# A first stage in units of two tiles that stores only z, with the transposed rows made during the walk

## The reference

```
xn   = (x - mean) / sqrt(var + 1e-5)                      # per row of x
neigh_mean = segment_sum(xn[src], dst) / max(deg, 1)      # 100000 edges, dst sorted
gnn  = relu(concat([xn, neigh_mean]) @ W + b), rows scaled to norm 1
mix  = linear attention of rmsnorm(xn) * g_pre:
       q, k, v = that @ w_qkv; softmax(k) over the nodes, softmax(q) over a head
       out = rmsnorm((context q) @ w_out + b_out, g_out) + xn
x    = x + gnn + mix
x    = x + moe(layernorm(x))                              # 8 experts, top 2, gelu
```

## Time and profile before

| | us |
|---|---|
| median of 3 executions | 2344.38 (2333.13 to 2353.49) |
| the profiled execution | 2353.81 |
| its span in the profile | 2352.2 |
| start of the first gather of the walk | 122.6 |
| first stage and tables: share of the span | 5% |

### The profile page before, as it was taken

The page is one execution under the profiler, slowest core; times in us unless marked ns, Lnnn a source line. Parts: engine busy times, 40 slices in busy tenths (PEclk is TensorE's granted clock), DMA queues, the critical chain, the costliest instruction groups (busy, mean ns, idle before and its releaser), DMA issues.

```text
span 2352.2 us, 34761 instructions
## 1 busy us (share of the span) xinstructions
PE 1657.8 (70%) x9472; PEld 1336.8 (57%) x9473; DVE 1372.5 (58%) x3837; ACT 594.3 (25%) x1554; POOL 1209.1 (51%) x1199
## 2 busy tenths in 40 slices
PE   2855666565556566787666544434999999999998
PEld 2633434343335344433434334424999999999997
DVE  7843444343335466776777567642666666666664
ACT  0200000000000133323433337521333333333332
POOL 4366676666666566656666534553333333333333
PEclk8966777677777777898787775556999999999999
DMA  7833333333332366666666547546776776777665
GB/s 212 283 104 98 99 105 100 98 103 101 103 103 81 115 222 197 200 177 187 200 196 191 164 122 258 181 131 158 197 200 194 191 199 197 190 194 200 196 188 152
DMA packets 203694, 387.28 MB, mean 165 GB/s; under 512 B 34677, under 2 KB 148362, under 8 KB 189015
## 3 DMA queue, kind: packets, MB, share of 16 engines
q0 software_dynamic: 77520, 258.14, 39.0%
q1 hardware_dynamic: 116448, 125.08, 17.0%
q10 hardware_dynamic: 9638, 3.13, 0.6%
HBM read 302.36 MB, written 84.67 MB: 165 GB/s over the span
## 4 chain that ended last, share of the span: by engine, by line
PE 48%; issue 15%; another core or an unknown queue 13%; DVE 12%; DMA 6%; POOL 3%; DVEq 1%; ACT 1%; SPq 1%; POOLq 0%; ACTq 0%
PE bank L1724 16%; PE bank L1574 11%; PE bank L1740 4%; PE bank L1742 4%; PE bank L1741 4%; DVE acc_lent L1156 4%; PE bank L1616 2%; DMA w1s<-in_x_dram 2%; PE bank L1582 1%; POOL G L626 1%; PE bank L1714 1%; PE bank L1631 1%; DMA xTs<-xnT_d 1%; POOL w2s_lent L626 1%
## 5 line engine op out<-in xcount | busy, mean ns | idle before, releaser
L1156 DVE TENSOR_TENSOR acc_lent<-acc_lent,bank 128x258 f32 x832 | 349.6, 420 | 531.0 <-remote 248.7
L626 POOL DMA_INDIRECT w2s_lent<-z_d,edge_tabs_lent x416 | 407.4, 979 | 234.5 <-issue 115.4
L626 POOL DMA_INDIRECT G<-z_d,edge_tabs_lent x416 | 408.6, 982 | 222.2 <-issue 118.1
L1574 PE MATMUL bank<-G,S_lent 128*128 128x258 f32 x832 | 308.3, 502 | 221.4 <-issue 114.3
L1724 PE MATMUL bank<-acc_lent 128*128 128x128 f32 x3392 | 398.2, 276 | 0.5 <-DVE acc_lent L1462 0.5
L1724 PEld LDWEIGHTS bank<-acc_lent 128*128 128x128 f32 x3392 | 390.2, 193 | 0.9 <-issue 0.9
L1574 PEld LDWEIGHTS bank<-G,S_lent 128*128 128x128 f32 x832 | 185.5, 245 | 333.6 <-issue 213.1
L909 ACT ACTIVATE G<-bank,acc_lent 128x128 f32<-128x128 f32 x848 | 242.6, 369 | 522.9 <-PE bank L1724 522.9
L1574 PE MATMUL bank<-w2s_lent 128*128 128x258 f32 x832 | 265.8, 447 | 129.3 <-issue 81.8
L1574 PEld LDWEIGHTS bank<-w2s_lent 128*128 128x128 f32 x832 | 163.6, 216 | 223.0 <-issue 152.7
L683 POOL DMA_INDIRECT out_dram<-acc_lent x106 | 170.4, 1607 | 187.5 <-DVE acc_lent L1468 172.9
(11 more groups left out here) (274 smaller groups left out, 2422.0 us busy)
## 6 DMA issues: line engine op xcount, KB each, us to landing
acc<-w2lo_d POOLq DMA_DIRECT2D x106, 1024.0 KB, 5.2
acc_lent<-bucket_d SPq DMA_DIRECT2D x106, 133.0 KB, 2.6
xTs<-xnT_d SPq DMA_DIRECT2D x98, 128.0 KB
bu_d<-w2s_lent SPq DMA_DIRECT2D x98, 128.0 KB
w2s_lent<-bu_d SPq DMA_DIRECT2D x14, 768.0 KB
w1s<-in_L_ffn_W_dram SPq DMA_DIRECT2D x8, 1024.0 KB
w2s_lent<-in_L_ffn_W_dram SPq DMA_DIRECT2D x32, 256.0 KB
w2hi_d<-w2s_lent SPq DMA_DIRECT2D x32, 256.0 KB
```

Source lines behind the costliest of these rows:

```text
L626: pool.indirect_dma_start(out=G_half[half][:, k, 0:D], out_offset=None, in_=z_d[:, :], in_offset=bass.IndirectOffsetOnAxis(ap=srcT[:, step ...
L1156: dve.tensor_tensor(to, to, bank[k % 4][:, 0:ACCW], ALU.add).then_inc(s["acc_done"], 1)
L1574: pe.matmul(bank[k % 4][:, 0:ACCW], S_half[half][:, k // S_GROUP, k % S_GROUP, :], G_half[half][:, k, :], start=True, stop=True).then_inc( ...
```

## The change

- **Units.** The first stage works on 25 units (LN_UNITS) of two tiles, with three buffers each for xn, xnT, zs. x is loaded by two tiles at a time with 8 loads outstanding (before: three tiles, 2 outstanding).
- **Who does what.** DVE writes mean and variance straight from bn_aggr, ACT's root adds eps through a bias pointer, DVE makes rstd and -mean*rstd (`scales`), and ACT normalises by an activation with scale and bias from pointers, one per tile. z is copied from PSUM by ACT for even units, by DVE for odd ones.
- **Stores.** Only z is stored in the first stage. POOL's additions and s_d are dropped.
- **Order at the start.** Units 0 to 5 (LN_BEFORE = 5) come ahead of the sort check. POOL clears acc after the 7 indirect DMAs. Of the weights only g_pre and w_kv are loaded here; ACT issues the other 17 DMAs one per tile in the first part of the walk, and DVE uses them in blocks 26 to 30 at step 3.
- **Walk, first part.** Per tile ACT normalises again from x_all (L706) into xr, PE transposes (`turn_a`, at step 2, two transposes), ACT copies into xTs (L806), and SP stores xTs to xnT_d (L435) where it loaded before.
- **Walk, last part.** SP loads x into sB; ACT makes s = x*(1 + rstd) - mean*rstd there (`make_s`), between `norm_o` and `copy_qT`; DVE waits for it.

The diff, cut to its core:

```diff
@@ first stage, SP
-            units(load_x, sp, None)
...
+            for n in range(LN_UNITS):
+                t0, nt = tiles_of(n)
+                until(sp, x_in[n % X_AHEAD], 16 * (n // X_AHEAD))
...
+            for n in range(9):
+                store_z(n)
...
-            def store_unit(i, h, t0, nt):
-                sp.wait_ge(pair["s_ready"][h], i + 1)
-                sp.dma_start(s_t[:, ds(t0, nt), :], ss[h][:, 0:nt, :]).then_inc(pair["s_out"][h], 16)
-                sp.wait_ge(pair["xnT_ready"][h], i + 1)
-                sp.dma_start(xnT_t[:, ds(t0, nt), :], xnT[h][:, 0:nt, :]).then_inc(pair["xnT_out"][h], 16)
...
             for t in range(NT):
+                sp.wait_ge(s["xa_ready"], t + 1)
+                sp.dma_start(xnT_d[t], xTs[:, :]).then_inc(s["xa_out"], 16)
@@ POOL
-            pool.memset(acc_flat, 0.0).then_inc(s["consts_pool"], 1)
...
             sort_places()
             step_rows()
-            with pool.Fori(1, UN) as i:
-                adds(i)
-            add_unit(UN, 0, NT - 1, 1)
+            pool.memset(acc_flat, 0.0).then_inc(s["consts_pool"], 1)
@@ ACT
+            def norm_x(to, t):
+                return act.activation(to, x_all[:, t, :], ACT.Identity, scale=rstd[:, t:t + 1], bias=mean_var[:, t, 0:1])
...
+            def ln_step(n):
+                if n + 1 < LN_UNITS:
+                    unit_sd(n + 1)
+                unit_xn(n)
+                if n >= 1:
+                    unit_xnT(n - 1)
+                if n >= 2 and n % 2 == 0:
+                    unit_z(n - 2)
...
             for t in range(NT):
+                if t < NT - 1:
+                    norm_a(t + 1)
                 kv(t)
+                if t < NT - 1:
+                    copy_a(t + 1)
+                next(weights, None)
...
+            def make_s(t):
+                act.wait_ge(s["sb_in"], 16 * (t + 1))
+                act.activation(sB[:, :], sB[:, :], ACT.Identity, scale=rstd1[:, t:t + 1], bias=mean_var[:, t, 0:1]).then_inc(s["s_made"], 1)
...
             def mix(t):
                 exp_q(t)
                 norm_o(t - 1)
+                make_s(t - 1)
                 copy_qT(t)
@@ DVE
-            def norm_iter(i, first=False, last=False):
-                norm_unit(i, 0, 6 * i, 3)
-                stats(i + 1, 0, 6 * i + 6, 1 if last else 3)
-                if not first:
-                    z_unit(i - 1, 0, 3)
...
+            for n in range(LN_BEFORE + 1, LN_UNITS + 1):
+                if n < LN_UNITS:
+                    stats(n)
+                if n % 2:
+                    z_unit(n - 2)
+                if n < LN_UNITS:
+                    scales(n)
+                if n == LN_BEFORE + 2:
+                    dve.wait_ge(s["kv_weights_in"], 16 * (DC + 1))
```

More of the change, by code:

```diff
@@ L456, in io_b @@
                     store_b(t - 1)
[L457 removed]
+                    load_s(t)
             def io_load(t, to, frm):
@@ new lines, in unit_sd, with unit_xn @@
+            def unit_sd(n):
+                t0, nt = tiles_of(n)
+                act.wait_ge(s["var_ready"], n + 1)
+                act.activation(rstd[:, t0:t0 + nt], mean_var[:, t0:t0 + nt, 1], ACT.Sqrt, bias=eps_ln).then_inc(s["ln_sd"], 1)
+            def norm_x(to, t):
+                return act.activation(to, x_all[:, t, :], ACT.Identity, scale=rstd[:, t:t + 1], bias=mean_var[:, t, 0:1])
+            def unit_xn(n):
+                t0, nt = tiles_of(n)
+                act.wait_ge(s["ln_ready"], n + 1)
+                until(act, s["xnT_mm"], n + 1 - LN_BUFS)
+                for tt in range(nt):
+                    a = norm_x(xn[n % LN_BUFS][:, tt, :], t0 + tt)
+                a.then_inc(s["xn_ready"], 1)
@@ new lines, in unit_xnT, with unit_z @@
+            def unit_xnT(n):
+                nt = tiles_of(n)[1]
+                h = n % LN_BUFS
+                act.wait_ge(s["xnT_mm"], n + 1)
+                until(act, s["z_mm"], n + 1 - LN_BUFS)
+                act.activation(xnT[h][:, 0:nt, :], x_bank[h][:, 0:nt * D].rearrange("p (t d) -> p t d", d=D),
+                               ACT.Copy).then_inc(s["xnT_ready"], 1)
+            def unit_z(n):
+                nt = tiles_of(n)[1]
+                h = n % LN_BUFS
+                act.wait_ge(s["z_mm"], n + 1)
+                until(act, z_out[h], 16 * (n // LN_BUFS))
+                act.activation(zs[h][:, 0:nt, :], z_bank[h][:, 0:nt * D].rearrange("p (t d) -> p t d", d=D),
+                               ACT.Copy).then_inc(s["z_copied"], 1)
@@ L777, in _ @@
                 act.dma_start(ed[0:EP], edges_d.rearrange("(p j) k e -> p j k e", j=EJ)).then_inc(s["edges_in_again"], 16)
-            repeat(act, None, copies, 1, UN - 1)
-            copy_xnT(UN - 1, 0, 3)
-            unit_sd(UN, 0, NT - 1, 1)
-            copy_xnT(UN - 1, 1, 3)
-            copy_xnT(UN, 0, 1)
-            act.wait_ge(s["rstd_ready"], 1)
-            act.activation(r16[:, :], t49, ACT.Sqrt).then_inc(s["sd_ready"], 1)
+            unit_sd(LN_BEFORE + 1)
+            for n in range(LN_BEFORE + 1, LN_UNITS):
+                ln_step(n)
@@ L787, in kv, with norm_a, copy_a @@
+            def norm_a(t):
+                until(act, s["xaT_mm"], t)
+                norm_x(xr, t).then_inc(s["xa_norm"], 1)
+            def copy_a(t):
+                act.wait_ge(s["xaT_mm"], t + 1)
+                until(act, s["kv_mm"], t)
+                until(act, s["xa_out"], 16 * t)
+                act.activation(xTs[:, :], bank[7][:, 0:D], ACT.Copy).then_inc(s["xa_ready"], 1)
             def kv(t):
@@ new lines, in stats, with scales @@
+                a.then_inc(s["var_ready"], 1)
+            def scales(n):
+                t0, nt = tiles_of(n)
+                r = rstd[:, t0:t0 + nt]
+                dve.wait_ge(s["ln_sd"], n + 1)
+                L.after(dve.reciprocal(r, r))
+                mean = mean_var[:, t0:t0 + nt, 0:1]
+                dve.scalar_tensor_tensor(out=mean, in0=mean, scalar=-1.0, in1=r.rearrange("p (t o) -> p t o", o=1),
+                                         op0=ALU.mult, op1=ALU.mult).then_inc(s["ln_ready"], 1)
@@ L1113, in _ @@
-            z_unit(UN, 0, 1)
-            rstd = mean_rstd[:, 1, 0:NT]
-            L.after(dve.tensor_tensor(t49, var49, rstd, ALU.mult))
-            L.after(dve.tensor_tensor(t49, t49, rstd, ALU.mult))
-            dve.tensor_scalar(t49, t49, float(D), None, ALU.mult).then_inc(s["rstd_ready"], 1)
+            for n in range(LN_BEFORE + 1):
+                stats(n)
+                if n >= 1:
+                    scales(n - 1)
+            scales(LN_BEFORE)
+            z_unit(1)
+            step_tables()
```

399 lines of the change are left out of this document (189 added, 210 removed).

## The result

The changed kernel takes 2386.7 us (median of 4, 2381.3 to 2392.3) against 2342.5 of the kernel before (four runs of it by now): ratio 1.020, interval 1.017 to 1.023. It is 44 us slower; 2375 was forecast.

A forecast was written before the change was run, and what follows sets the result against it. It took the old first stage's steady part as DVE-bound at 1.50 us a tile, the walk as bound by no single engine. Stage 14, clock 8, clearing 4, walk 1 and 4 gave +31 on 2344.4: 2375 us, range 2325 to 2410.

The forecast's parts named there:

- The chain: First stage's loop: steps wait on one another round all engines, 8.25 us a pair of units, no engine full.
- The rival that the loop isn't a chain: First stage's loop: signals overlap, PE bounds at 2.42 us a unit; total 2330 to 2325 us; chance 0.16.
- The stage's sum: First stage: its pieces add up to a first gather at 136.4 us against 122.6, +14 us.
- The forecast's own sign: End of first stage: the walk's first gather would show at 136 us, within 123 to 165.
- The start: Before the loop: PE's sort check matmul stands behind five units, at 35.4 us, 9.1 later; DVE resumes at about 44.9.
- The clearing: POOL's clearing of acc, now inside the first stage's loop, may hold DVE's scaling of w_kv: +4 us, bounds 0 and +10.9.
- Clock: First stage's loop: PE's idle time in each pair lowers its granted clock: +8 us, bounds 0 and +25.
- Half clock throughout: Rival: PE stays at 1.2 GHz in the whole first stage, pair 11.0 us, total 2392 us; chance 0.10.
- The first round: First stage, after DVE resumes: unit 6 through its first round, charged as half a pair, 4.4 us.
- The tables: First stage's loop: casting and subtracting steps, 0.6 and 1.45 us, plus two pairs of table copies of 1.76: 5.6 us.
- The walk: After the first stage: added transposes and normalisations +1 us in its first part, making s +4 in its last.
- that rival (2300): Walk's first part gets faster without xTs's load, up to 74 us back, total 2300 us; chance 0.14.

The follow-up runs named there:

- the best version: Changed kernel with clearing at start, odd z copy later, normalisation before root, LN_BEFORE 3, earlier W_neigh load, tables' steps spread: 2134.0 us (0.995), again 2128.7 (0.994).
- the filled version: Changed kernel with 6 extra, unused PE matmuls at even steps of the first stage's loop, not at the tables' steps: 2187.8 us, ratio 1.020.
- the version with the three edits: Changed kernel with acc cleared at the start, odd units' z copy one step later on DVE, ACT's normalisation ahead of the next root: 2341.3 us, ratio 1.0005.
- the version with the late z copy: Changed kernel with DVE copying z of odd units one step later, acc clearing left late: 2352.4 us, ratio 1.004.

## Why the prediction was right, point by point

- **The chain: right, and shown.** Forecast 8.25 us a pair, measured 8.07 at full clock. That the lengths agree to 0.2 is partly luck, since the forecast added 2.75 us of PE to two rounds of DVE and ACT, and the trace shows 4.7 us of PE and one round. Moving one copy made it 5.90, moving the root as well 4.92. The rival that the loop isn't a chain (2325 to 2330) falls: its first gather of 103 is approached only once the order is edited (113.1, and 104.1 and 106.3 in the best version).
- **The stage's sum: 136.4 forecast, 168.2 measured, with clock and clearing 148.** The forecast's own sign, a first gather from 123 to 165, was missed. The start is 3.1 late: PE waited 6.9 us for W_neigh, which the forecast had landed by 18.4, though the five units then took 13.0 and not 17. Its load was issued at 13.98 and took 11.7 us, where it was issued at 11.0 before and took 7.1; why it took longer was not tested. From DVE's return to its first z copy it is 8.5 and not 4.4. The nine intervals between z copies (56.50 to 163.65) take 107.2 against 74.3 + 5.6. The end is 2.6 shorter.
- **The clearing: mechanism right, term too small.** +4 forecast inside bounds of 0 and 10.9; the multiply was held for 11.05, 10.4 more than its 0.61. It began 0.2 us behind the clearing, so nothing of it was over: the argument that DVE would come late to it was a guess.
- **Clock: right in kind, mis-sized where the loop had long pauses.** +8 was forecast. Outside of the tables' pairs I count 9: 1.6 ahead of the first z copy (PE's part of that way is 4.1 us and 2.5 at full clock), 2.5 behind the clearing, and 5.0 in three of the last five pairs, beside the filled version. In the tables' pairs PE's pieces of the chain take 19.1 us; by the plain pairs and by the best version's transposes of the steps (0.93 for seven) they would take about 11 at full clock, an estimate. So the clock took some 17 us in all, twice the charge. Half clock throughout (2392) did not come to be, since pairs at full clock stand among the others, and its nearness to 2386.7 is luck.
- **The first round: charged half a pair, 4.4.** It takes 8.5, of which 1.6 is the clock. DVE and ACT go through two rounds before PE may start on the newest unit, so 2.5 were missing; the scaling's own 0.6 stood in no term either.
- **The tables: the step that failed.** I charged their own work, 5.6 us, and left them out of the chain. DVE's wait for PE's transposes of the steps stands ahead of the next unit's statistics, as the z copy does. The two pairs take 19.8 and 12.9 us, 16.6 over two plain pairs, so 11 beyond the charge. By the estimate above some 8 of the 11 are the low clock of these two pairs and 3 are the wait and the transposes on PE; that the pauses brought the low clock is argued here, since these pairs were filled only in part. Other profiles of the same stage show 30.3 to 32.7 us for the two, so 9 to 11 beyond the charge. In the version with the three edits, at full clock, the tables cost 3.3 beyond it. Apart by two units and behind the loop's slack they cost the best version 5.5, which is the charge.
- **The walk: charged 5, measured 0 to 3.** Its first part did not get faster either (564.7 to 564.2 us), though xTs's load left it: that rival (2300) falls, and the load was not what holds the blocks at 12 us. What does was not looked for.
- **The total.** Sum of the terms as measured: 14 + 3 (start) + 3 (first round and scaling) + 10 (clearing, on +0) + 9 (clock) + 11 (tables, 8 of it clock) - 3 (end), less 2 for the shorter pairs, gives the 45.6 at the gather within rounding; the median shows 44.3. The forecast of +31 was right in sign and held by its range. It held in part by luck: the stage alone was 20 us over its terms, and the 5 us charged for the walk were not needed.

## What to carry to other kernels

When work moves from the bounding engine to idle ones, write down what each engine's list waits for over two iterations, and add up the longest way round: busy shares of 57, 51 and 38% hid a loop that no engine bounded, and the place of one copy was worth 27 us, or 34 with the collision that it happened to avoid. An instruction that waits for the newest result of another engine should stand behind all work that doesn't need it, by one iteration more. A wait placed inside such a loop for a side job (here the tables) joins the chain, so its price is the chain's, not its own, and a pause of PE that it makes can cost clock as well. An edit of the order also moves what meets what on other engines: compare it with a version in which that collision is gone.

## What the runs showed of the hardware

- Two DVE multiplies of 128x256 took 11.05 us together beside POOL's clearing of 128x12900 words (10.86), and 0.61 without it; the compare to a 128x128 bf16 or f32 tile at the start was held in the same way (9.85, 9.98). A product of two SBUF operands of two columns, issued 0.14 us into the clearing, took its usual 0.16, and so did the four such products that the version with the late z copy ran beside its clearing. The Trainium skill ("GPSIMD Engine Reference", section 1, Specifications) says that POOL and VectorE contend when VectorE is in a two-port mode or reads two operands from SBUF. The small product, which by it would have been held in every unit, was not held in these five cases; no row shows the mode in which the multiplies ran.
- PE with more than half as much work again (7.23 us a pair in place of 4.64) was faster per loop: in pairs with 2.7 us of matmuls of no use in the gap the clock stayed at 1.00 and the pair at 8.07; without them some of these pairs took 9.7 at 0.82. The Trainium skill ("TensorE: Matmul & The Clock Gate", Part 1) says of the clock gate that activity releases the clock, and these pairs agree. But gaps of 3.4 us in each 8.07 did not keep it low in the pairs from 78.1 and from 118.9, where it was 1.00.
- The first and the third chip differ by 14% in the first part of the walk (564.7 and 486.9 us for the same stretch of the kernel before) and by 8.5% in the whole, at a mean PE clock of 0.817 and 0.865, but hardly in the first stage (122.6 and 121.3 us). Why was not looked for.
